# Three edits to the order of work in a fused attention and expert layer: one weight split, one PSUM bank, five choosing steps

## What is computed

```python
mod = (_silu(c) @ wmod).reshape(8, 6, 1, -1)      # sa, ca, ga, sb, cb, gb
h = _layernorm(x) * (1 + ca) + sa
x = x + ga * attention(h, w_q, b_q, w_k, b_k, w_v, b_v, w_o, b_o)   # 16 heads of 32, causal
h = _layernorm(x) * (1 + cb) + sb
x = x + gb * ffn(h)

def ffn(h):                                       # h is 8192 x 512 as rows
    scores = sigmoid(h @ gate_w.T)                # 32 experts in 8 groups
    # per token: best 4 groups by the sum of their two best biased scores, of these the best 4 experts
    topk_idx, topk_w = route_tokens(scores, bias)
    pos = place of each (token, expert) pair in its expert's queue    # a running count over tokens
    # pairs with pos < 256 go through the expert; h = relu(x up)**2 @ down, weighted by topk_w
    return routed + relu2(h @ shared_up.T) @ shared_down.T
```

## Time and profile before

| what | us |
|---|---|
| median of 3 runs | 3001.86 (2996.71 to 3007.34) |
| the profiled execution, its own time | 3024.03 |
| its span | 3022.3 |
| PE busy in the span | 2920.5 (97%) |
| DVE / POOL / ACT busy | 2117.6 / 1837.8 / 1343.0 |

### The profile page before, as it was taken

How to read it: one execution, slowest core, us unless ns; L and a number is a source line. 1 busy time by engine, 2 the same in 40 slices (tenths; PEclk the granted TensorE clock), 3 DMA queues, 4 the chain that set the end, 5 groups by cost and what they waited for, 6 DMA issues and landing times. The chain is left out here.

```text
span 3022.3 us, 49806 instructions
## 1 busy us (share of the span) xinstructions
PE 2920.5 (97%) x16480; PEld 2169.3 (72%) x16480; DVE 2117.6 (70%) x5344; ACT 1343.0 (44%) x2436; POOL 1837.8 (61%) x1077
## 2 busy tenths in 40 slices
PE   8999999999999999999999899999999999989997
PEld 5788888766666666666666577787877888768775
DVE  6555555677777777777777586787878888856764
ACT  2222222166666666666666532323332233226764
POOL 1332223278788887888878146567665776655664
PEclk9999999999999999999999999999999999999998
DMA  7555555755655566555664332233323332248996
GB/s 257 195 203 193 184 180 177 236 113 134 134 128 115 121 134 135 122 115 125 135 138 121 125 112 74 81 102 109 98 74 109 101 99 81 74 132 213 234 235 119
DMA packets 281948, 420.53 MB, mean 139 GB/s; under 512 B 48463, under 2 KB 132687, under 8 KB 281742
## 3 DMA queue, kind: packets, MB, share of 16 engines
q1 hardware_dynamic: 259214, 384.22, 44.7%
q0 software_dynamic: 22528, 33.72, 5.8%
HBM read 263.38 MB, written 153.01 MB: 138 GB/s over the span
## 5 line engine op out<-in xcount | busy, mean ns | idle before, releaser
L1165 ACT ACTIVATE att_pt<-att_ps_p 128x512 f32<-128x512 f32 (+1 forms) x1024 | 524.8, 586 | 142.6 <-PE att_ps_p L1388 118.2
L247 DVE CUSTOM_DVE_ANT_0 att_ps_s<-att_ps_s,att_causal 128x512 f32<-128x512 f32 (+1 forms) x992 | 470.0, 503 | 137.2 <-PE att_ps_s L1303 136.9
L1385 PE MATMUL att_ps_p<-att_qs,att_ks 98*128 98x512 f32 (+3 forms) x1536 | 505.3, 369 | 8.2 <-ACT att_pt L1165 7.8
L1303 PE MATMUL att_ps_s<-att_ks,att_qs 96*128 96x512 f32 x1488 | 508.2, 370 | 2.2 <-DVE att_lower L253 0.6
L253 DVE TENSOR_REDUCE att_lower<-att_ps_s 128x1 f32<-128x512 f32 x496 | 339.9, 685 | 115.1 <-PE att_ps_s L1303 115.0
L1104 POOL TENSOR_TENSOR att_gathered<-att_gathered,att_pt 128x2048 f32<-128x2048 f32 (+1 forms) x92 | 388.4, 4222 | 41.2 <-ACT att_pt L1165 36.4
L1385 PEld LDWEIGHTS att_ps_p<-att_qs,att_ks 98*128 98x128 f32 x1536 | 272.2, 191 | 152.7 <-issue 106.0
L1097 POOL TENSOR_TENSOR att_pt<-att_pt 128x1024 f32<-128x1024 f32 (+2 forms) x153 | 331.3, 2165 | 70.2 <-PE att_ps_o L1329 52.5
L1911 POOL DMA_INDIRECT slot_info<-ffn_info,ffn_slot x256 | 276.1, 1078 | 113.5 <-issue 78.7
L1303 PEld LDWEIGHTS att_ps_s<-att_ks,att_qs 96*128 96x128 f32 x1488 | 275.2, 191 | 68.5 <-DVE att_rowmax L247 22.1
L577 POOL TENSOR_TENSOR qkv_x<-qkv_x,qkv_mod 128x512 f32<-128x512 f32 x60 | 83.5, 1392 | 368.1 <-DVE qkv_x L671 368.1
(11 more groups left out here) (311 smaller groups left out, 6558.4 us busy)
## 6 DMA issues: line engine op xcount, KB each, us to landing
att_qs<-qk_parts SPq DMA_DIRECT2D x96, 512.0 KB, 6.8
att_ks<-qk_parts SPq DMA_DIRECT2D x96, 512.0 KB, 12.8
qk_parts<-qkv_out_hi SPq DMA_DIRECT2D x128, 256.0 KB, 2.2
qk_parts<-qkv_out_lo SPq DMA_DIRECT2D x128, 256.0 KB, 2.4
qkv_x<-x SPq DMA_DIRECT2D x16, 1024.0 KB, 5.4
v_rows<-qkv_out_v SPq DMA_DIRECT2D x64, 256.0 KB, 2.3
att_vs<-v_rows SPq DMA_DIRECT2D x32, 512.0 KB, 16.0
o_parts<-att_o SPq DMA_DIRECT2D x64, 256.0 KB, 7.5
```

Of the source, the lines that this page charges most:

```text
L247: dve.tensor_tensor_reduce(part, part, self.causal[:, UNIT - (c1 - c0):UNIT], scale=1.0, scalar=MASKED, op0=ALU.add, op1=ALU.max, accum_ou ...
L1165: act.activation(tile(c)[:, h, col:UNIT], ps_p[(NPROB * prev.g + n) % NP][:, col:UNIT], ACT.Exp, scale=float(HD) ** -0.5).then_inc(exp_don ...
L1303: pe.matmul(bank("s", cur.g, i)[:, 0:c1 - c0], qs[cur.slot][0:STACK, h, t * P:(t + 1) * P], ks[cur.slot][0:STACK, h, c0:c1], start=True, s ...
L1385: last = pe.matmul(part[:, i * (UNIT - col):(i + 1) * (UNIT - col)], ks[prev.slot][:, h + i, kt * P:(kt + 1) * P], qs[prev.slot][:, h + i, ...
```

## The change

The first piece moves the split of the first weight on DVE behind both modulation halves. The second puts the last three softmax sums into the fourth bank, `ps_s[3]`, by three empty uses in the ring, so that the projection's spare banks are 0 to 2; PE's wait for the last copied sum then moves from ahead of the first transposes to ahead of unit 0's logits. The third takes unit 0's choosing steps 3, 4 and 5 from in front of `attend` and puts step 3 behind the DVE work of down sum 1 and steps 4 and 5 behind that of down sum 2; `places(0)` on PE moves from in front of the down sums to behind them.

```diff
--- before.py
+++ after.py
@@ -708,13 +708,13 @@
             for t in range(UT):
                 xt = x_sb[0][:, t, :]
                 dve.tensor_tensor(xt, xt, mod[:, 1, :], ALU.mult).then_inc(mul_done, 1)
-            low_weights(0)
             dve.wait_ge(first_done, 2)
             dve.tensor_copy(mod[:, 0, :], ps_m[1][:, :])
             dve.drain()
             for t in range(UT):
                 xt = x_sb[0][:, t, :]
                 dve.tensor_tensor(xt, xt, mod[:, 0, :], ALU.add).then_inc(h_done, 1)
+            low_weights(0)
             for k in range(DK):
                 low_turned(0, 0, k)
             take_pair(0, ps_m[2][0:2 * LANE, :])
@@ -961,8 +961,10 @@
                         ring.append(("sum", g - 1, 1))
         last_sums = [(GROUPS - 2, 1), (GROUPS - 1, 0), (GROUPS - 1, 1)]
         SCORES = len(ring)
-        ring = ring + [use for g, qh in last_sums for use in (("sum", g, qh), None, None, None)]
-        SPARE = [ps_s[(SCORES + 1 + i) % NS] for i in range(NS - 1)]
+        LAST_BANK = NS - 1
+        assert SCORES % NS == 0
+        ring = ring + [None] * LAST_BANK + [use for g, qh in last_sums for use in (("sum", g, qh), None, None, None)]
+        SPARE = ps_s[0:LAST_BANK]
         PROJECT = {c: c - TOTAL_AT[1] for c in range(TOTAL_AT[1], TOTAL_AT[1] + UT)}
         PLACE = {use: n for n, use in enumerate(ring) if use}
 
@@ -1723,7 +1725,7 @@
         SCATTERED_AHEAD = TOPK
         CHOSEN_AHEAD, PLACED_AHEAD = {0: (0, 1), 1: (2,), 2: (3,), 3: (4, 5)}, 4
         DOWN_AT = {0: 0, 1: 1, 3: 2, 4: 3}
-        FIRST_CHOICE = {1: (1,), 5: (2,), 7: (3, 4, 5)}
+        FIRST_CHOICE, FIRST_CHOICE_LATE = {1: (1,), 5: (2,)}, {1: (3,), 2: (4, 5)}
 
 
         def steps(eng, body):
@@ -2173,6 +2175,9 @@
                     if more:
                         for t2 in TURNS[t]:
                             low_turned(u + 1, t2)
+                    if u == 0:
+                        for step in FIRST_CHOICE_LATE.get(t, ()):
+                            choose(u, step)
                 if u < UNITS - 2:
                     give_slots(u, half)
 
@@ -2233,7 +2238,6 @@
                     last = pe.transpose(ps_g[:, 2 * t * NE:2 * (t + 1) * NE], gateT_sb[:, t * P:(t + 1) * P], ident[0:2 * NE, 0:2 * NE])
                 last.then_inc(gate_done, 1)
 
-            pe.wait_ge(bridge.t_free, CREDIT + QH * GROUPS)
             for t in range(UT):
                 turn(0, t)
 
@@ -2242,6 +2246,7 @@
                 first = isinstance(u, int) and u == 0
                 pe.wait_ge(lo_done, CREDIT + UT * (u + 1))
                 if first:
+                    pe.wait_ge(bridge.t_free, CREDIT + QH * GROUPS)
                     pe.wait_ge(bridge.o_free, CREDIT + QH * GROUPS)
                     pe.wait_ge(w_lo_done, CREDIT + NW_UP)
 
@@ -2269,7 +2274,7 @@
                     places(u)
                 if more:
                     project(*((b, 1) if half == 0 else (b + 1, 0)), lambda t: pe.wait_ge(relu_done, CREDIT + UP * u + UP - RING + t + 1))
-                if u < UNITS - 2:
+                if 0 < u < UNITS - 2:
                     places(u)
 
                 if more:
@@ -2294,6 +2299,8 @@
                     if more:
                         for t2 in TURNS[t]:
                             turn(u + 1, t2)
+                if u == 0:
+                    places(u)
 
             steps(pe, body)
             experts.tensor(pe)
```

## The result

The changed kernel takes 3015.02 us (median of 20 runs, 3004.48 to 3026.07), the kernel before 3005.75 us (20 runs beside them, 2994.76 to 3017.53). The ratio is 1.0028, with a 95% interval of 1.0016 to 1.0040: **8.4 us slower, between 4.8 and 12.0** (the two medians differ by 9.3). Single runs of either kernel spread over more than 20 us, so one profile of each does not show the difference: the profiled execution of the changed kernel has a span of 3005.9 us, the one of before 3022.3. What a profile does show is the length of single stages. (PE is TensorE, DVE VectorE, ACT ScalarE and POOL GpSimd. Of this kernel lines from 965 on are 2 higher than before, in TensorE's part 5: L1994 was L1992, L2214 was L2209.)

What follows compares the result with a forecast made beforehand. PE is busy 97% of the span, so edits gain only from its idle or low-clock time. The three edits sum -1.1 + 0 + 0.4 = -0.7 us on 3001.86, giving 3001.2 us, range 2994.8 to 3006.3.

Steps and rivals of the forecast that it cites:

- First edit: Start, weight split behind both modulation halves: first `low_turned` and first projection matmul come 1.1 us earlier.
- Second edit: Change from attention to last stage: PE's 2.45 us wait moves behind the transposes, as ACT is not free; gain 0.
- Third edit: Unit 0, moved choosing steps: one 4.95 us wait becomes two, about 0, plus 0.4 us for POOL contention.
- the first wait: Unit 0, PE behind down sum 1, for POOL's first tile: shrinks from 4.95 to 1.8 us, low clock behind it.
- step 3 at 3.5 us plus 0.4 for contention: Unit 0, DVE: step 3 takes 3.5 us as before; POOL normalising beside its two such operations adds 2 x 0.18.
- The wait in down sum 3: Unit 0, middle of down sum 3: PE newly waits 2.8 us for `low_turned(1, 1)`, with the low clock behind it.
- One reading of the clock: Unit 0, behind the 1.8 us wait: clock falls, 8 matmuls at the low level cost 1.6 us, hidden by DVE.
- rival 4: Unit 0: DVE and POOL hold each other up, step 3 blocked at full price; +1.9 us, 3003.8; chance 0.14.
- Rival 1: Unit 0: the waits change places and the clock still falls; 3001.2 us; chance 0.55.
- Rival 2: Unit 0, down sum 3: clock stays up in the second wait, saving 2.0 us; -2.7, 2999.2 us; chance 0.22.
- Rival 3: All three places: all the waiting goes, as the edits read; -12.2 us, 2989.7; chance 0.06.
- Rival 5: Whole kernel: edits do nothing lasting, only code lying elsewhere in memory; within 1 us of the median; chance 0.03.

Runs made afterwards that it cites:

- before_copy: The kernel before, unchanged, run again on the chip of changed_third, held_second and early_held; 3005.52 us, ratio 0.9998, unit 0 68.30 us.
- no_choice: The changed kernel without the third edit, so the first two edits on the kernel before; ratio 1.0000 to before, unit 0 68.82 us.
- changed_third: The changed kernel itself, measured a third time, on the chip of before_copy; 3013.50 us, ratio 1.0018 to before, unit 0 71.05 us.
- early_held: The changed kernel with step 3 back in front of `attend` and POOL held until unit 0's third addition; 3008.64 us, ratio 1.0000 to before.
- block_pool_held: The kernel before plus 14 unused DVE multiplications in unit 0, with POOL held until they are over; 2997.53 us, ratio 1.0038 to before.
- held_second: The changed kernel with POOL held until unit 0's third addition, measured a second time; 3005.34 us, ratio 0.9986 to before.
- changed_again: The changed kernel itself, measured again on the chip of the first POOL-held kernels; 2992.33 us, ratio 1.0010 to before.

## Why the prediction was wrong

The four comparisons of kernels with step 3 in front of the addition gave 1.0028, 1.0023, 1.0010 and 1.0018; weighted by the inverse squares of their intervals that is 1.0020, 6.0 us, with an interval of my own from the same weights of 3.7 to 8.4. The two with POOL held give 0.9997 in the same way. I forecast -0.7 us with a range of -7.1 to +4.4 around the median I had; the first comparison gave +8.4. The median of before itself was 3.9 us above that of my three runs, which is not the change's; without it the result is still 3011.1, above the range's end of 3006.3.

**First edit, forecast -1.1.** Its steps held: transposes at 22.62 (22.9 forecast), first `low_turned` at 24.55 (24.85), first projection matmul 1.37 us earlier. What the sum left out is the clock. In all ten profiles with this edit the granted clock is below 1 between 28 and 32 us, in only three of the eight without it. In the changed kernel the window from 28 to 32 has 0.60, by estimate a loss of 4 x 0.4 = 1.6 us. Without the edit the low clock came at this place too, in before_copy at 0.50 through the whole window, so it is not the edit's alone. What is left of the lead at the end of stage one can be read: the last matmul of its kind (L844, high by high part) starts at 601.0 to 602.6 in the ten profiles with the edit, at 600.8 to 601.7 in the five without it whose clock held, and at 603.0 to 605.0 in the three whose clock fell. Alone the edit measured 0.9992 (0.9978 to 1.0006), which holds both nothing and the forecast.

**Second edit, forecast 0.** The rows agree, and for the reason given: ACT's list held. The times agree within their width only: 1.0007 alone (0.9989 to 1.0025), and `no_choice` at 1.0000 (0.9978 to 1.0022) has it inside.

**Third edit, forecast +0.4.** The frame was right: `attend` stood 3.8 us closer to the last low part (1.35 us behind it against 5.14 in the earlier trace rows; 4.0 forecast), the first wait shrank, a new one rose in the middle of down sum 3, and the low clock stood behind it. **The term that failed is step 3 at 3.5 us plus 0.4 for contention.** Step 3 took 5.0 us, and the addition behind it 1.49, for which I had 1.24 and which takes 0.69 undisturbed. From `attend` to the end of `low_turned(1, 1)` that made 32.5 us in place of the forecast's 30.7, so 1.8 us where I had 0.4. A second, smaller term was off too: counted from the gate copy, `attend` came 3.2 us earlier, not 4.0. Unit 0 grew by 2.3 us. The four profiles with step 3 in this place and POOL free have 71.05 to 71.66 us; the five of kernels whose unit 0 is that of before have 68.30 to 69.59; the means differ by 2.3 us, the two on one chip by 2.75. The wait in down sum 3 was 3.4 to 4.5 us in the four, not 2.8, and in all four the comparison took 1.81 or 1.82 us and the addition 1.49. The first wait did not shrink to the 1.8 us forecast (2.75 and then 1.20 us here; 3.3 to 4.5 in the other three).

I had read the contention off the median of L2172, 0.18 us over its least. But a median over 16 units says how often the two engines meet, not what a meeting costs; at this place POOL is at work without a break, and the longest value was the one to take. POOL's work there was also not the normalising that I named, which had ended at 1779.80, but the products of the attention output behind it, which start earlier once `attend` does.

One reading of the clock failed as well, at no cost: I took it to fall behind the first wait. Behind 2.75 us it did not (1.00 in the two windows from 1774 to 1776), behind the 3.49 us of changed_third it did (0.50 from 1774 to 1775), and either way the wait for DVE hid it.

That is **rival 4**, to which I gave 0.14. Its mechanism is shown by 14 operations (1.32 against 0.76 us) and in the changed kernel on two chips (waits of 3.42 against 2.13 us and of 4.48 against 1.98); its size, +1.9 forecast in all, measured +2.3 to +2.9 in unit 0. The condition that it names was met: DVE lost 1.5 us in step 3 and 0.8 in the addition, over 1.1.

The Trainium skill (SBUF — State Buffer, "Who interferes with whom") says which VectorE operations GpSimd can hold up: those with two SBUF inputs, where GpSimd's own reads SBUF, and casts in a two-port mode, but never a `tensor_reduce` on this chip. The rows of step 3 agree: beside POOL the comparison takes 1.81 us and the cast 0.61, without it 0.69 and 0.17, while the reduction takes 1.04 and 1.08. The product `picked` has two SBUF inputs as well and took 0.68 in both; it began as POOL's product ended, and POOL's cast beside it took 0.88 us, where an undisturbed one takes 0.61. I quoted the rule and then set it at 0.14, on the strength of a median.

**Rival 1**, waits that change places, is what is left once POOL is held: unit 0 at 67.8 to 68.3 us, the time level. **Rival 2** is refuted here, as the clock was at 0.50 behind the second wait. **Rival 3** did not come, nor did `early_held` bring a part of it. **Rival 5**, code that lies elsewhere, is not supported for the sign: ten comparisons of kernels with other code and step 3 elsewhere, or POOL held, have ratios of 0.9986 to 1.0008 (`block_pool_held`, with its added work, left out).

**What is not settled.** Unit 0 explains 2.3 to 2.9 us. On the chip without the long stalls the change cost 3.0 us (-0.9 to 7.2), which that covers. On the others it cost 8.4, 6.9 and 5.4 us. Weighted as above that is 7.5 us, with 4.7 to 10.3 as my estimate of the interval, so some 3 to 6 us come on top there that unit 0 does not show (about 2 at the interval's lower end). What makes them is open. It goes when POOL is held (held_second is level) or step 3 stands elsewhere, on chips with the same stalls, so it seems to hang on the same place; whether by unit 1's stalls, single profiles can't tell. Unit 1's stalls are where I would look.

## What to carry to other kernels

Price a moved VectorE operation by what GpSimd does beside its new place: if GpSimd works there without a break, take the longest duration of the same form, not the median. Before moving steps off the front of a chain, find what stands next in the engine's list at their new place and which engine waits for it; here one addition further on cost nothing measurable (+2.4 and -0.9 us, each give or take 4 to 5), and in front of it cost 6 us. A dose (fourteen such operations in one place) shows in six runs whether its price is made good later, where an effect of 0.2% needs dozens.

## What the hardware showed that I had not expected

- **Stalls that belong to the chip or the occasion.** On one chip every unit from 1 to 13 took 59.2 us in all four profiles (unit 1 twice 59.3 and once 59.5), and the kernel before took 2988.18 us; on the others units 1 and 8 often took 60 to 70 us and it took 3005 to 3008. `changed_again` ran on that chip, and the stall of unit 1 that the changed kernel's first profile has was not there (59.27 us against 67.86). Windows of the same stretch, of the changed kernel first and then of changed_again (the third number from the end is the clock):

```profile
1820.00:1830.00 10.00, 9.54 (x29) 0.67 0.01 3
```

```profile
1820.00:1830.00 10.00, 10.00 (x46) 1.00 0.02 3
```

- **A delay in unit 0 reached the end in full, as far as the intervals tell.** 18.5 us of work in front of one addition lengthened unit 0 by 18.5 us and the program by 18.6 (13.2 to 24.0). 14 operations of 0.76 us (10.64) lengthened it by 9.7 us over the first profile of before and the program by 11.4 (6.6 to 16.1).
